# Issue order on the Sync and GpSimd engines in a fused attention and expert kernel

## The reference

```python
x = x + cross_attention(layernorm(x), ctx, ctx, mask)   # 16 heads of depth 16, softmax over 256 keys
x = x + ffn(layernorm(x))
# ffn: softmax router over 8 experts, top 2, capacity 1024 rows an expert,
#      h = silu(a) * g with (a, g) = rows @ c_fc[e]; out = h @ c_proj[e], weighted, summed over the 2
```

## Time and profile before

| what | value |
|---|---|
| median of 3 runs (lowest, highest) | 466.27 us (464.39, 466.72) |
| time of the profiled execution | 467.2 us |
| span of the profiled execution | 465.4 us |
| PE busy | 384.8 us, 83% of the span |
| DVE, ACT, POOL busy | 250.1, 211.8, 165.3 us |
| Sync's hardware DMA queue | 44.82 MB, 40.0% of 16 engines' span |

### The profile page before, as it was taken

The page is one execution under the profiler, slowest core; times in us unless marked ns, Lnnn a source line. Parts: engine busy times, 40 slices in busy tenths (PEclk is TensorE's granted clock), DMA queues, the critical chain, the costliest instruction groups (busy, mean ns, idle before and its releaser), DMA issues.

```text
span 465.4 us, 9282 instructions
## 1 busy us (share of the span) xinstructions
PE 384.8 (83%) x2713; PEld 296.4 (64%) x2714; DVE 250.1 (54%) x694; ACT 211.8 (46%) x340; POOL 165.3 (36%) x174
## 2 busy tenths in 40 slices
PE   4546695996979969896979677979999999999990
PEld 3424463664655646563544346869999999999980
DVE  4544664585977868686876545463333323332330
ACT  2512363564455554563444154634445445444540
POOL 5021042521556435535050404163233333333332
PEclk9969798898988989898785659799999999999997
DMA  5578478392882928539060249534433234324440
GB/s 168 151 158 167 132 171 185 105 199 88 166 236 74 225 103 167 144 117 196 3 212 28 90 174 282 115 76 64 69 59 52 46 62 68 56 43 66 65 57 4
DMA packets 67514, 54.02 MB, mean 116 GB/s; under 512 B 11898, under 2 KB 64394, under 8 KB 67466
## 3 DMA queue, kind: packets, MB, share of 16 engines
q1 hardware_dynamic: 60076, 44.82, 40.0%
q0 software_dynamic: 7008, 8.43, 10.7%
q10 hardware_dynamic: 400, 0.40, 0.3%
HBM read 32.89 MB, written 21.18 MB: 116 GB/s over the span
## 4 chain that ended last, share of the span: by engine, by line
PE 60%; DMA 13%; DVE 8%; issue 6%; SPq 5%; ACT 4%; POOL 2%; ACTq 0%; POOLq 0%; DVEq 0%
PE bank L979 21%; PE bank L990 10%; PE bank L830 7%; DMA wf<-NMT 6%; PE bank L934 6%; PE bank L905 4%; PE bank L918 3%; PE bank L866 2%; DVE NEG L1107 2%; PE bank L839 2%; SPq L414 2%; SPq L429 2%; DMA qparts_d<-QP 2%; DMA kparts_d<-KP 2%; PE bank L959 2%
## 5 line engine op out<-in xcount | busy, mean ns | idle before, releaser
L1107 DVE TENSOR_REDUCE NEG<-bank 128x2 f32<-128x512 f32 x128 | 85.7, 684 | 51.6 <-PE bank L905 48.7
L979 PEld LDWEIGHTS bank<-CX,KS 128*128 128x128 f32 x912 | 109.1, 194 | 5.9 <-issue 3.8
L979 PE MATMUL bank<-CX,KS 128*128 128x128 f32 x912 | 109.8, 278 | 2.9 <-issue 2.8
L728 ACT ACTIVATE PR<-bank 128x512 f32<-128x512 f32 x128 | 73.4, 590 | 71.1 <-PE bank L918 70.1
L635 POOL DMA_INDIRECT out<-CTt,GG x38 | 58.9, 1550 | 101.3 <-DMA out<-CTt,GG 81.1
L763 ACT ACTIVATE KS<-wf 128x1536 f32 x40 | 59.2, 1483 | 47.1 <-PE bank L979 29.6
L905 PE MATMUL bank<-KS,wf 99*128 99x256 bf16 x224 | 45.7, 290 | 23.6 <-DVE NEG L1107 15.7
L1339 DVE COPY CX<-bank 128x256 f32<-128x256 f32 x39 | 16.5, 424 | 77.9 <-PE bank L959 59.3
L990 PE MATMUL bank<-wp,QF 128*128 x228 | 57.1, 388 | 0.8 <-DVE CTt L1353 0.8
L918 PE MATMUL bank<-wf,KS 102*128 102x256 bf16 x224 | 46.6, 291 | 9.6 <-DMA wf<-NMT 8.8
L572 POOL DMA_INDIRECT slots<-R,slot x32 | 32.2, 1005 | 61.5 <-DVE slot L1213 50.8
(11 more groups left out here) (170 smaller groups left out, 465.4 us busy)
## 6 DMA issues: line engine op xcount, KB each, us to landing
wf<-in_L_ffn_c_fc SPq DMA_DIRECT2D x8, 768.0 KB
XG<-slots SPq DMA_DIRECT2D x40, 128.0 KB
slots<-pad_row SPq DMA_DIRECT2D x8, 387.0 KB
kparts_d<-KP SPq DMA_DIRECT2D x8, 384.0 KB, 2.5
KS<-kparts_d SPq DMA_DIRECT2D x8, 384.0 KB
KS<-kparts_d SPq DMA_DIRECT2D x24, 128.0 KB
qparts_d<-QP SPq DMA_DIRECT2D x8, 384.0 KB, 3.1
wp<-in_L_ffn_c_proj SPq DMA_DIRECT2D x8, 384.0 KB
```

What stands on the lines that cost most here:

```text
L728: act.activation(PR[:, s % NPROB, :], STB[s % 2][:], ACT.Exp).then_inc(exp_done, 1)
L979: ins = pe.matmul(bank[2 + 2 * u + g][:, c * P:(c + 1) * P], UP[u][:, (k * 2 + g) * FF + c * P:(k * 2 + g) * FF + (c + 1) * P], XTG[:, u, ...
L1107: dve.tensor_reduce(NEG[:, n % 2, t, 2 * hp:2 * hp + 2], MXB[m % 2][:].rearrange("p (i s) -> p i s", i=2), AX.X, ALU.max, negate=True).the ...
```

## The change

Four things move. (1) Sync issues `max_rows(it + 1, 0)` before the context and the expert weights of the same iteration, not after them; `load_context` moves from the head of an iteration to the end of the one before. (2) POOL does `scatter(it - 2)` ahead of `layernorm2(it - 1)` in all iterations from 2 on. (3) In the prologue the rows of batch 2 are loaded right after `wv`; the rows of batch 3 and the context of batch 2 are issued between the write of K and the write of Q of batch 1; K of batch 1 is read back after its Q is written; the rows of batches 4 to 7 are loaded after `load_rest`. (4) In the table: batch 1's projections start a unit later (7), batch 2's start 4 units before iteration 0 where it was 7, and `NM0` moves from unit 11 to unit 10.

```diff
-    "second K of the first": 2, "second Q of the first": 8, "start of 1": 6, "lead": 7,
-    "NM0": 11, "NM1": 2, ...
+    "second K of the first": 2, "second Q of the first": 8, "start of 1": 7, "lead": 7, "lead of 2": 4,
+    "NM0": 10, "NM1": 2, ...
@@ start_unit
-    return UNITS * -2 + n * AT["start of 1"] if n < 2 else UNITS * (n - 2) - AT["lead"]
+    if n < 2:
+        return UNITS * -2 + n * AT["start of 1"]
+    return UNITS * (n - 2) - (AT["lead of 2"] if n == 2 else AT["lead"])
@@ Sync, prologue
             sp.dma_start(wv[:], ...)
+            load_rows(2)
@@ Sync, loop
             for it in ITERATIONS[:-1]:
-                if 3 <= it + 3 < B:
-                    load_context(it + 3)
                 if 0 <= it < B:
                     max_rows(it, 1)
...
                     write_parts(n, KP, kp_ready, kd_out, kparts_d)
-                    if n < 2:
+                    if n == 0:
                         read_rows(n, KS[:, n % 3], ROWS3, 0, MATCH_K, kd_out, kparts_d)
+                    if n == 1:
+                        load_rows(3)
+                        load_context(2)
                     write_parts(n, QP, qp_ready, qd_out, qparts_d)
-                    if n >= 2:
+                    if n >= 1:
                         read_rows(n, KS[:, n % 3], ROWS3, 0, MATCH_K, kd_out, kparts_d)
                     read_rows(n, query_rows(n), 0, ROWS3, MATCH_Q, qd_out, qparts_d)
-                    if n == 0:
-                        load_rows(2)
-                        load_context(2)
-                    if n == 1:
-                        for m in range(3, B):
-                            load_rows(m)
...
+                if 0 <= it + 1 < B:
+                    max_rows(it + 1, 0)
+                if 3 <= it + 4 < B:
+                    load_context(it + 4)
                 if 0 <= it < B:
                     ... load_up, wp ...
-                if 0 <= it + 1 < B:
-                    max_rows(it + 1, 0)
                 if it == -1:
                     load_rest()
+                    for m in range(4, B):
+                        load_rows(m)
@@ GpSimd, loop
-                if it >= B - 2:
+                if 0 <= it - 2:
                     scatter(it - 2)
                 if 0 <= it - 1:
                     layernorm2(it - 1)
-                if 2 <= it < B - 2:
-                    scatter(it - 2)
```

## The result

| | before | after |
|---|---|---|
| median (lowest, highest), 4 runs each | 466.5 us (464.39, 469.3) | 452.72 us (451.31, 454.1) |
| ratio, 95% interval | | 0.9696 [0.9653, 0.9739] |
| profiled execution, its span | 467.2, 465.4 us | 451.36, 449.6 us |

The change makes the kernel 13.8 us faster; the forecast was 13.3 us, 453.0 us. The profiled spans differ by 15.8 us. A later pair of timings came out smaller: 0.9839 [0.9772, 0.9906]. The last experiment is about that. Medians in this document are over all runs of a kernel, while ratios leave out runs more than 1.5% above its fastest; the profiled executions of two kernels, all but the scatter (459.68 us) and both repairs (471.71 us), are such slower runs.

A forecast was written before the change was run, and what follows sets the result against it. The prediction took PE's waits in the first 294 us, mainly for maxima queued behind expert weights, as all that can change. 6.2 + 4.6 + 2.5 + 0 = 13.3 us off 466.3 gave 453.0 us, range 445 to 461.

The forecast's parts named there:

- up to iteration 1: Prologue and iteration 0: Sync 3.4 us earlier plus 2.8 us for maxima not behind weights, 6.2 us, bounds 1 to 9.
- iteration 1 to the start of 2: Start of iteration 2: the 3.53 us `NMT` wait goes, plus 1.1 us of lower clock, 4.6 us, bounds 2 to 5.5.
- iterations 2 to 4, maxima: Starts of iterations 3 and 4: PE's DMA waits of 0.6 and 1.9 us go, 2.5 us, bounds 1 to 4.
- iterations 2 to 4, scatter: Iterations 2 to 5: moving POOL's scatter ahead of `layernorm2` changes nothing, 0 us, bounds +6 to -5.
- rival A: Prologue: half 1 waits behind other loads and Sync for Q's parts; worth 1 to 3 us, 457 to 458 us, chance 0.16.
- The yardstick: Iteration 6, already in the new scatter order, against iteration 5 in the old: 16.97 against 16.38 us, taken as 0.
- 2.44 us stop: DVE's idle stretch before row maxima at 134.75, seen in iterations 2 to 5; said it may follow the late scatter.
- Rival B: Iterations 2 to 5: the early scatter helps, about 1.2 us or more each; 448 us, chance 0.17.
- they just fit into that wait: Iteration 2: the scatter's four indirect DMAs, 5.1 us, fit POOL's 5.07 us wait for `stats2`, so nothing is late.
- rival D: Iterations 2 to 5: `rs2` late behind the scatter holds DVE and so PE; slower than before, 471 us, chance 0.04.
- rival C: Iterations 2 to 5: early scatter beside K and Q reads, and port cost, add 1.5 us each; 459 us, chance 0.12.
- signs that I had named for a wrong prediction: `normalize2` waiting over 1 us for POOL, a long stop at `logits(0, 8)`, or DVE's stall growing at its new place.

The follow-up runs named there:

- The last experiment: The kernel before, the changed kernel unaltered and both repairs, timed together in a later series: 472.41, 466.08 and 466.82 us.
- all but the scatter: The changed kernel with the scatter put back behind `layernorm2` in iterations 2 to 5: 457.02 us, ratio to before 0.9741.
- both repairs: The changed kernel with the output bias added one iteration later and iteration 5's scatter put back behind `layernorm2`: 466.82 us, ratio to before 0.9752.
- the maxima alone: The kernel before with only half 0's maxima and the context issued ahead of the expert weights and `NM0` in unit 10: 455.53 us, ratio 0.9760.
- the changed kernel run again: The changed kernel, unaltered, timed and profiled once more in a later series: 466.08 us, ratio to before 0.9839.
- the prologue alone: The kernel before with only the prologue's new load order and the new starts of batches 1 and 2: 465.19 us, ratio 0.9945.
- twice the scatter: The kernel with the maxima alone, each of the scatter's indirect DMAs issued a second time into a spare buffer: 501.39 us in one run.

## Why the prediction was right, and where it was not

| term | forecast | measured, profiled spans |
|---|---|---|
| up to iteration 1 | 6.2 | 4.2 (78.91 to 74.74) |
| iteration 1 to the start of 2 | 4.6 | 6.0 (108.67 to 98.50, less 4.2) |
| iterations 2 to 4, maxima | 2.5 | 7.4 together (193.66 to 176.07, less 10.2) |
| iterations 2 to 4, scatter | 0 | in the row above |
| iterations 5 and later | 0 | -1.8 |
| sum | 13.3 | 15.8 |

The forecast's total was right in part by cancellation: the prologue gave less than its term, iteration 1 to 2 more, and a gain of the scatter in iterations 2 to 4, for which I had 0, stands against a loss in iteration 5 and after. By the experiments the maxima alone are worth 11.1 us, where the prediction's parts for them add up to 2.8 + 4.6 + 2.5 = 9.9.

**The maxima.** Right. `NMT` waits of iterations 2 to 5 are gone and Q's eight matmuls take 1.96 us, as forecast. The stop itself gave 3.4 us (V of iteration 1 to the start of 2). What I missed is at the other end of the iteration: it opened at the lower clock behind its own stop, 7.7 us from 78.91 to V at 86.61, and takes 5.1 now (74.74 to 79.87), which is 2.6 us. These hang on this one profile, in which PE has no long stop for the query rows: with the maxima alone, where it stops 3.18 us for them, the stretch takes 7.0 us (76.81 to 83.84), and 8.0 in the changed kernel run again (75.94 to 83.90). So they are luck of the profiled execution rather than the work of the maxima. The 1.1 us that I had for the clock behind the stop at 2 came out as 0.5 (V of 2 is 10.7 us earlier, the start 10.2). Of the 7.4 us in iterations 2 to 4 the maxima have 3.3, for my 2.5: from V of 2 to V of 5 it is 85.38 us before, 82.07 with the maxima alone and 77.57 after.

**The prologue.** Mis-sized. DVE's 6.06 us for batch 3's rows are gone. Iteration 0 begins 3.5 us earlier (52.73 to 49.25), not 6: `max_rows(0, 0)` goes out at 42.54, inside my 41.5 to 43.6, and what follows it takes as long as I counted, but `max_rows(0, 1)` then goes out at 56.36 where I had 55.1 by counting from the early end. So Sync gives 2.2 us in place of 3.4 there. The term behind it is off as well: I had the parts of batch 2 ready near 57.5, so that Sync would find them, but it writes K only at 59.87, after a wait, which is 1.6 us earlier than before (61.51); that is rival A's mechanism at a small size. Of the 2.8 us for the maxima DVE keeps some back: PE waits 1.23 us for it just ahead of iteration 1, at 74.52. The stall at `logits(0, 8)` is 1.51 us for my 2, and is missing when the changed kernel is run again. The other bound is the query rows: "I take no loss, but no slack is left" was the right worry. PE waits for them at iteration 1 in nearly every run, and between the two profiles of the changed kernel V of iteration 1 moves by 4.0 us (79.87 to 83.90), 1.4 of them by the later start and the rest by the slower matmuls behind the stop.

**The scatter, iterations 2 to 4.** The step that failed is the 0. The yardstick, iteration 6 against 5, has no reads and no splits of K and Q, and its weights go out at 237.58, after the scatter, so it could show neither the 2.44 us stop nor what POOL's bias add and split do at the old place. What I left out was `ls` held by POOL's bias add. Against the kernel with the maxima alone the move is worth 1.0, 1.8 and 1.8 us in iterations 2, 3 and 4. Together that is 4.5 us in the table's distances, and the kernel with all but the scatter agrees. Rival B had the size about right for these three iterations, but by luck: it named the 2.44 us stop, and in the kernels that the gain is measured against the stop isn't there (DVE waits 0.45 us); what goes is the hold of `ls`.

**Iteration 5.** The scatter costs something here, up to 3.5 us against the maxima alone (28.65 to 25.20). The prediction's step "they just fit into that wait" held even so: the slots come late, POOL waits 4.43 us for them, and it is still done 0.28 us before the statistics. So rival D's mechanism, `rs2` late behind the scatter, did not run. What ran is the part of rival C that I had called "inside the yardstick": the bias add beside `normalize2` (1.68 us for 0.73), 1 us of waiting for PE, and the lower clock behind it. B's gain of 4.5 and this loss of 3.5 leave 1.0 us, so my 0 was nearly right by cancellation.

**Iterations 5 and later** are a row of -1.8 us. V of 5 is 0.9 us nearer to the start than before; from V of 5 to V of 6 it is 1.4 us longer; the last 1.3 are behind that, where the wait for `R` in iteration 7 is 4.18 us in place of 3.00. Why that one grew is open.

**The port.** The Trainium skill, SBUF — State Buffer, section "SBUF: two separate sides", has the rule that VectorE in a two-port mode, or with two inputs in SBUF against a GpSimd operation that reads it, and GpSimd lock each other out for whole instructions. The traces agree: 1.68 to 2.51 against 0.72 us for `R`, 1.82 to 2.39 against 0.17 for `ls`. By that rule alone four iterations would lose 3.7 us; measured was a hold of 1.0 us in each of iterations 2 and 5, and none in 3 and 4, where the bias add is over in time.

**Rival C** ran on the chip of the last experiments: the stop of 2.8 to 3.2 us in three iterations, which with the low clock behind it makes them 30 us, longer than the 27.3 to 29.3 of the kernel before in its profile. There the ratio of 0.984 would be what the maxima and the prologue leave, which is argued and not shown. That ACT and DVE would be the ones to start late, and not the reads, I had not foreseen. Two of the signs that I had named for a wrong prediction are so in part there: a stop at `logits(0, 8)` in the first profile (1.51 us) and a stall at the new place on this chip (PE waits 2.8 to 3.2 us). What differs between the chips is open: no trace of the kernel before was taken on that one.

## What to carry to other kernels

A small transfer that the next stage waits for belongs ahead of bulk loads in its queue; this alone was 11 of the 14 us. Before moving a step to a new place in a loop, list for every iteration what runs beside it and beside the steps that it pushes away, at the old place and the new one, small operations too: here three of four iterations gained and the fourth gave much of it back, both by an operation of VectorE held beside one of GpSimd. And before a stop is put down to a pair of transfers, look for it in every kernel that has the pair. A gain of a few us that hangs on which transfers coincide should be timed on more than one chip.

## What the runs showed of the hardware that was not expected

- ACT and DVE can start together on work that PE's rows show as done 2 to 3 us before (134.73 and 134.75 in the kernel before, 121.95 and 121.99 in the changed kernel run again). The scatter's packets and dense traffic of the hardware queue are both there each time, but kernels with the same pair go without the stop (0.45 us in the prologue alone, the maxima alone and all but the scatter). With twice the scatter PE stood 2.9 to 4.0 us at that place. Beside the K and Q reads it came on one chip, in three kernels, and not in the early-scatter kernels profiled elsewhere. The cause is open.
- A DVE operation of 16 numbers a partition can take 2.39 us in place of 0.17, when POOL works on two tensors in SBUF.
- A stretch of 3 us in which the K and Q reads were under way in row order moved 128 to 133 GB/s with all DMA engines busy; loads of the weights beside them reached 294 GB/s in the earlier trace rows.
- The same kernel pair gave 0.9696 and 0.9839 in two series, and the kernel before alone took 466.5 to 466.7 us in three series and 472.4 us on the chip of the last.
